# Masked decay products and FFN weight preparation of a Mamba-2 + NVFP4 kernel moved from GpSimd to ScalarE, VectorE and TensorE

## The reference

```
zxbcdt = u @ W_in                      # 256 -> z 512, x 512, B 128, C 128, dt 8
xBC = silu(causal_conv4(xBC))          # 4 taps along the tokens
dt = softplus(dt + dt_bias); A = -exp(A_log); dA = A * dt       # one per token and head
L = exp(segsum(dA))                    # decay between tokens, lower triangle
y = (C B^T * L) @ (x * dt)  + what earlier tokens leave behind  + D * x
y = rmsnorm(y * silu(z)) @ W_out;  h = layernorm(u + y)
W[k] = LUT[4-bit code] * scale[block of 32]                     # gate, up (2048x256), down (256x2048)
out = layernorm(h + (gelu(h @ Wg.T) * (h @ Wu.T)) @ Wd.T)
```

## Time and profile before

| | |
|---|---|
| median of 3 runs | 1005.04 us (1004.16 to 1058.38) |
| the profiled execution | 1005.52 us, its span 1003.8 us |
| TensorE busy | 920.3 us, 92% of the span |
| VectorE busy | 722.4 us, 72% |
| ScalarE busy | 457.8 us, 46% |
| GpSimd busy | 268.1 us, 27% |
| start to 85 us | the first group |
| 85 to 205 us | group 0 with the first group's MLP (front half to 130 us) |
| 205 to 868 us | groups 1 to 6, 110 to 111 us each |
| 868 to 1004 us | the last group, and its MLP |

### The profile page before, as it was taken

The page is one execution under the profiler, slowest core; times in us unless marked ns, Lnnn a source line. Parts: engine busy times, 40 slices in busy tenths (PEclk is TensorE's granted clock), DMA queues, the critical chain, the costliest instruction groups (busy, mean ns, idle before and its releaser), DMA issues.

```text
span 1003.8 us, 15853 instructions
## 1 busy us (share of the span) xinstructions
PE 920.3 (92%) x5416; PEld 803.8 (80%) x5416; DVE 722.4 (72%) x1334; ACT 457.8 (46%) x788; POOL 268.1 (27%) x264
## 2 busy tenths in 40 slices
PE   5558678899999999999999999999999999999997
PEld 4437577888888889888888888888888889978887
DVE  7957867687767876687758786687859766776453
ACT  4534334454544445354545445445445554444332
POOL 4633643203412133203402232203411322111000
PEclk9797778999999999999999999999999999999999
DMA  4011100010001000010001000010001000000000
GB/s 134 26 55 57 36 1 9 15 53 1 1 22 43 21 0 21 0 63 0 0 21 62 1 0 21 0 63 0 21 0 63 1 1 12 25 29 1 1 33 11
DMA packets 18793, 23.11 MB, mean 23 GB/s; under 512 B 1728, under 2 KB 15296, under 8 KB 18752
## 3 DMA queue, kind: packets, MB, share of 16 engines
q1 hardware_dynamic: 18176, 22.56, 7.1%
q10 hardware_dynamic: 576, 0.03, 0.0%
HBM read 14.19 MB, written 4.19 MB: 18 GB/s over the span
## 4 chain that ended last, share of the span: by engine, by line
PE 43%; issue 34%; POOL 13%; DVE 7%; ACT 1%; DMA 1%; POOLq 0%; SPq 0%; DVEq 0%; ACTq 0%
POOL uT_lo L1103 4%; PE mixer L471 4%; PE mixer L472 4%; PE mixer L473 4%; PE up_bank L471 3%; PE gate_bank L471 3%; PE up_bank L472 3%; PE up_bank L473 3%; PE gate_bank L473 3%; PE gate_bank L472 3%; PE mixer L550 3%; PE down L471 2%; PE down L472 2%; PE down L473 2%; POOL uT_hi L1103 2%
## 5 line engine op out<-in xcount | busy, mean ns | idle before, releaser
L471 PE MATMUL down<-wd_hi,in_hi 128*128 128x256 f32 x512 | 145.7, 285 | 0.7 <-DVE in_lo L1000 0.7
L1103 POOL TENSOR_TENSOR uT_hi<-tri,dA_hi 128x1024 fp32r<-128x1024 f32 x30 | 59.2, 1973 | 323.5 <-DVE dA_lo L867 182.1
L472 PE MATMUL down<-wd_lo,in_hi 128*128 128x256 f32 x512 | 145.2, 284 | 0.0
L473 PE MATMUL down<-wd_hi,in_lo 128*128 128x256 f32 x512 | 145.0, 283 | 0.0
L883 DVE SCALAR_TENSOR_TENSOR xbc<-mixer,chan,xbc 128x510 f32<-128x510 f32 (+1 forms) x162 | 110.9, 685 | 27.1 <-ACT xbc L680 24.7
L738 ACT ACTIVATE in_hi<-act_sb 128x512 fp32r<-128x512 f32 (+1 forms) x144 | 83.6, 581 | 94.1 <-PE down L473 55.5
L752 ACT ACTIVATE act_sb<-gate_bank 128x512 f32<-128x512 f32 (+1 forms) x144 | 79.2, 550 | 103.1 <-PE gate_bank L473 101.3
L471 PE MATMUL up_bank<-hT_hi,wu_hi 128*128 128x512 f32 (+1 forms) x288 | 109.2, 379 | 11.2 <-DVE act_sb L1014 11.2
L471 PE MATMUL gate_bank<-hT_hi,wg_hi 128*128 128x512 f32 (+1 forms) x288 | 116.7, 405 | 2.3 <-ACT act_sb L752 2.3
L1000 DVE TENSOR_TENSOR in_lo<-act_sb,in_hi 128x512 fp32r<-128x512 f32 (+1 forms) x144 | 107.0, 743 | 15.7 <-ACT in_hi L738 15.7
L1014 DVE SCALAR_TENSOR_TENSOR act_sb<-up_bank,act_sb 128x512 f32<-128x512 f32 (+1 forms) x144 | 90.1, 625 | 31.6 <-PE up_bank L473 25.7
(11 more groups left out here) (205 smaller groups left out, 2078.2 us busy)
## 6 DMA issues: line engine op xcount, KB each, us to landing
xbc<-in_u_t_dram SPq DMA_DIRECT2D x7, 512.0 KB, 3.6
h_sb<-in_u_dram SPq DMA_DIRECT2D x7, 512.0 KB, 3.9
h_res<-h_sb SPq DMA_DIRECT2D x7, 512.0 KB, 2.9
out_dram<-h_res SPq DMA_DIRECT2D x7, 512.0 KB, 2.9
scales<-in_ffn_s_dram SPq DMA_DIRECT2D x24, 128.0 KB, 2.2
packed<-in_ffn_w_dram SPq DMA_DIRECT2D x8, 96.0 KB, 2.0
xbc<-in_u_t_dram SPq DMA_DIRECT2D x2, 256.0 KB, 2.8
xbc<-in_W_in_dram SPq DMA_DIRECT2D x1, 512.0 KB, 6.2
```

Source lines behind the costliest of these rows:

```text
L471: nc.tensor.matmul(dst, lh, rh, start=first, stop=False, skip_group_check=True)
L472: nc.tensor.matmul(dst, lh, rl, start=False, stop=False, skip_group_check=True)
L473: return nc.tensor.matmul(dst, ll, rh, start=False, stop=last, skip_group_check=True)
L1103: ins = tt(R, mask, f32(step[:, i, :]).unsqueeze(2).to_broadcast([P, H, P]), ALU.mult)
```

## The change

ScalarE forms both parts of the masked dA, each by eight copies of 128x128 with a scale taken from `dA_hi` or `dA_lo` (16 for a tile, 512 in all); GpSimd's two instructions for a tile go. TensorE now waits for two semaphores, `R_h` and `R_l`. VectorE multiplies codes and scales (`value`) for all 24 chunks. The rest of chunks 12 to 23 is formed as that of the first 12 is, by TensorE (in bank `OB[1]`, the second bank of the down products) and ScalarE. The tables of steps are written anew. GpSimd keeps the lower part of uT, the small steps of the norms and the splits of `W_in`'s z part and of `W_out`, the latter two now in four pieces each, the z part only after the first tap of x4.

```diff
-                elif kind == "R":
-
-                    if i:
-                        wait_ready(pool, f"D{i - 1}b", g)
-                    elif kind_of(g) != "first":
-                        wait_ready(pool, "z3" if tiles(g) == 4 else "x3", g)
-                    wait(pool, dA_ok, g, 1)
-                    mask = tri[:, :].unsqueeze(1).to_broadcast([P, H, P])
-                    for R, step in zip(R_of(g), (dA_hi, dA_lo)):
-                        ins = tt(R, mask, f32(step[:, i, :]).unsqueeze(2).to_broadcast([P, H, P]), ALU.mult)
-                    ins.then_inc(R_ok.sem, 1)
...
+                elif kind == "R":
+                    wait_R(act, i, g)
+                    for R, step, done in zip(R_of(g), (dA_hi, dA_lo), (R_h, R_l)):
+                        for h in range(H):
+                            ins = nc.scalar.activation(R[:, h, :], tri[:, :], ACT.Copy, scale=f32(step[:, i, h:h + 1]))
+                        ins.then_inc(done.sem, 1)
...
-                    wait(pe, R_ok, g, i + 1)
+                    wait(pe, R_h, g, i + 1)
+                    wait(pe, R_l, g, i + 1)
...
+            def value(c):
+
+                block, third = c // 3, c % 3
+                code = codes[:, block % 2, :, :].bitcast(FP8)[:, :, third * CW:(third + 1) * CW]
+                dve.wait_ge(decoded.sem, block + 1)
+                dve.wait_ge(scales_in[c % 2].sem, 16 * (c // 2 + 1))
+                if c >= 2:
+
+                    dve.wait_ge(wt_rest.sem, c - 1)
+                if c == BESIDE_FIRST + 1:
+
+                    wait_ready(dve, "Y1", FIRST)
+                tt(chunk_out(c), code, scales[:, c % 2, :].unsqueeze(1).to_broadcast([P, 2, CW]),
+                   ALU.mult).then_inc(valued.sem, 1)
...
-            def rest(c):
-                hi, lo = prep_dst(c)
-                pool.wait_ge(wt_hi.sem, c + 1)
-                tt(lo, chunk_out(c), f32(hi), ALU.subtract).then_inc(wt_lo_pool.sem, 1)
...
-VALUE = {FIRST: {"x5": [2], "R0": [3], "R1": [4, 5, 6, 7, 8, 9, 10, 11]},
...
+VALUE = {FIRST: {"x0": [2], "x1": [3], "x2": [4], "x3": [5], "D0": [6], "XT0": [7], "XT1": [8], "Y1": [9],
+                 "gT0": [10], "op0": [11]},
...
```

More of the change, by code:

```diff
@@ L57 @@
[L57 to L63, removed]
+BESIDE_FIRST = 12
+DECODE = {FIRST: {"x1": [2], "XT0": [3], "gT0": [4]}, 0: {"x5": [5], "x1": [6], "x3": [7]}}
@@ new lines @@
+VALUE = {FIRST: {"x0": [2], "x1": [3], "x2": [4], "x3": [5], "D0": [6], "XT0": [7], "XT1": [8], "Y1": [9],
+                 "gT0": [10], "op0": [11]},
+         0: {0: [12], "x0": [13], 1: [14], "z1": [15], "x2": [16], 3: [17], "z3": [18], "CB0": [19], 5: [20],
+             6: [21], "XT1": [22], "D1": [23]}}
+UPPER = {FIRST: {"x1": [2], "z0": [3], "z1": [4], "CB0": [5], "D1": [6], "Y0": [7], "Y1": [8], "gT0": [9],
+                 "op0": [10], "gT1": [11]},
+         0: {"x5": [12], "z0": [13], "x1": [14], 2: [15], "z2": [16], "x3": [17], 4: [18], "XT0": [19], "D0": [20],
+             "Y0": [21], 7: [22], 8: [23]}}
@@ new lines @@
+TAKE_OFF = {FIRST: {"x5": [0], "x0": [1], "z0": [2], "x2": [3], "x3": [4], "D0": [5], "Y0": [6], "XT1": [7],
+                    "gT0": [8], "op0": [9], "gT1": [10], "op1": [11]},
+            0: {"x0": [12], 1: [13], "z1": [14], "x2": [15], 3: [16], "z3": [17], "CB0": [18], 5: [19], 6: [20],
+                "XT1": [21], "D1": [22], "Y1": [23]}}
+LOWER = {FIRST: {"x1": [0], "z0": [1], "z1": [2], "x3": [3], "CB0": [4], "D1": [5], "XT1": [6], "Y1": [7],
+                 "op0": [8], "gT1": [9], "op1": [10], "ln1": [11]},
+         0: {"z0": [12], "x1": [13], 2: [14], "z2": [15], "x3": [16], 4: [17], "XT0": [18], "D0": [19], "Y0": [20],
+             7: [21], 8: [22], "XT2": [23]}}
@@ L317, in wait_bank, with wait_R @@
                 wait(eng, s, g - 1, k)
+        def wait_R(eng, i, g):
+            if i:
+                wait_ready(eng, f"D{i - 1}b", g)
+            elif kind_of(g) != "first":
+                wait_ready(eng, "z3" if tiles(g) == 4 else "x3", g)
+            wait(eng, dA_ok, g, 1)
         def f32(ap):
@@ L623, in prep @@
             def prep(g, item):
[L624 to L627, removed]
+                for c in TAKE_OFF[g].get(item, ()):
+                    b = chunk_bank(c)
                     pe.wait_ge(valued.sem, c + 1)
                     if c >= 4:
-                        pe.wait_ge(wt_lo_act.sem, c - 3)
+                        pe.wait_ge(wt_lo.sem, c - 3 if c < BESIDE_FIRST else c)
                     nc.tensor.matmul(b[:, :], ident[:, :], chunk_out(c), start=True, stop=False, skip_group_check=True)
@@ L768, in prep @@
                     upper(c)
-                if kind_of(g) == "first":
-                    for c in LOWER.get(item, ()):
-                        lower(c)
+                for c in LOWER[g].get(item, ()):
+                    lower(c)
             def any_mixer(name, g):
@@ L1045, in decode @@
                 tt(lower, word, lower, ALU.bitwise_or).then_inc(decoded.sem, 1)
+            def value(c):
[9 more added lines that the diff above has]
+                   ALU.mult).then_inc(valued.sem, 1)
             def prep(g, item):
+                for c in VALUE[g].get(item, ()):
+                    value(c)
                 for b in DECODE[g].get(item, ()):
@@ L1058, in _ @@
             decode(0)
+            value(0)
+            value(1)
             dve.wait_ge(win_top.sem, 1)
@@ L1153, in any_mixer @@
                     pool.wait_ge(wout_top.sem, 1)
[L1154 removed]
+                    for j in range(JT):
+                        tt(wout_lo[:, j, :], wout_raw[:, j, :], f32(wout_hi[:, j, :]), ALU.subtract)\
+                            .then_inc(wout_ok.sem, 1)
                 mixer(name, g)
```

69 lines of the change are left out of this document (21 added, 48 removed).

## The result

The changed kernel takes **1009.7 us** (median of 6 runs, 1009.1 to 1010.0) against 1006.4 of the kernel before (median of 6, which counts a slow run of 1058.4 us; the five others have a median of 1005.5): the ratio without that run is 1.0035, with a 95% interval from 1.0018 to 1.0052. 984 us were forecast, in a range from 970 to 1009. The profiled execution has a span of 1007.4 us, 3.6 us more than before's 1003.8.

What follows compares the result with a forecast made beforehand. TensorE bounds steady groups, VectorE's queue, held up by GpSimd, group 0's front half. From 1005.5 us: 2 (first 85 us), 10 and 6 (group 0's front half, head part) and 3.5 (steady groups) off, 984 us; range 970 to 1009.

Steps and rivals of the forecast that it cites:

- R's price: ScalarE's scaled 128-column copies for R: 0.30 us apart, 4.8 us a tile, bounds 0.22 and 0.40 us a copy.
- Rivals 1 and 2: ScalarE's R copies: not overlapping, 0.40 us each, 1010 us (chance 0.14); or ScalarE bounding the head part, about 1040 us (0.06).
- So a steady group gets 0.5 us shorter: Steady groups: the wait for W shrinks with R on ScalarE; six groups and the last one gain 3.5 us.
- TensorE still busy over 98% of a steady group: Sign in the new profile's steady groups; below 97% ScalarE's queue, and the prediction with it, would be priced wrong.
- the four rivals: Whole kernel: copies not overlapping (0.14), ScalarE bounding the head part (0.06), group 0 hardly gaining (0.22), everything gaining (0.12).
- The front half of group 0, -10: Group 0 before its head part: VectorE's queue relieved by net 9.5 us, 10 us gained, bounds 3 and 14.
- 14 matmuls of 0.23 us, 3 us, go into its 14 us of waits: Group 0's front half: TensorE's added chunk matmuls, 3 us, would fit inside its existing waits.
- rival 3: Group 0 hardly gains, as chunks go round in-order engines and TensorE stops at each: 3 us and 0 there, 998 us; chance 0.22.
- The head part of group 0, -6: Group 0's later part: earlier W and faster Y, less 4 us for R1 and chunk steps; 6 us gained, bounds 0 and 9.
- The first 85 us, -2: Start of the kernel: VectorE freed of GpSimd, against new products and R on ScalarE; 2 us gained, bounds 6 gained, 3 lost.
- R0 and R1 eat 5 to 7 of it: First 85 us: convolutions end 6 us earlier, and the first group's R copies on ScalarE use up 5 to 7 us.

Runs made afterwards that it cites:

- after_pad64: The changed kernel with 128 long-satisfied waits (64 instructions) ahead of VectorE's first wait for the channels, no loop instruction altered; 1001.9 us.
- best: The changed kernel with the first group's R on GpSimd, rests of chunks 12 to 23 subtracted by VectorE, and spare waits spread over idle places; 981.5 us.
- r_only: The kernel before with R made by ScalarE's 16 copies a tile, the chunks staying with GpSimd; 996.9 us.

## Why the prediction was wrong

All four terms of the sum had the wrong size, two of them the wrong sign. By its own steps:

- **R's price was right.** 0.29 us apart (forecast 0.30), 390 ns long, 4.68 us a tile (4.8); D0 late by 0.56 us (0.5), Y0's wait gone, VectorE's `in_lo`, `tail` and `xtail` at 0.68, 0.17 and 0.69 us. The budget of the Trainium skill's page "ScalarE: Activation LUTs", section "Rules for kernel authors", which comes to an estimated 0.41 us, is near what the row shows as a duration, 0.39 us; as a distance it is 0.12 us too much. Rivals 1 and 2 didn't happen.
- **"So a steady group gets 0.5 us shorter"** was right for every second group and a quarter of the truth for the others. The step failed in counting the wait for W as its 1.42 us alone; the windows of before show 1.7 us of slow clock behind it in every second group. Without the idle stretches (after_pad64) groups 1 to 6 take 659.1 instead of 667.3 us: 8.2 us where I had 3.
- **"TensorE still busy over 98% of a steady group"** (97.6% was measured) failed on something that I had not priced at all. I took the groups that the diff doesn't touch as changed by R only. The chunk products moved VectorE's loop in its program, and it was fetched again at each turn: 4 times some 2.1 us, and 1.7 us more in group 5, where TensorE's granted clock was 0.91 on average for 20 us (667 to 687) around the wait. Together 669.1 - 659.1 = 10.0 us. This is the largest single part of the miss, and it isn't in any of the four rivals.
- **The front half of group 0, -10.** VectorE's relief came as worked out (cut by stage from 42.6 to 32.5 us busy, 10.0 where I had 9.5), and TensorE's two waits for it, 14 us, went to 1. What failed is the sentence that TensorE's "14 matmuls of 0.23 us, 3 us, go into its 14 us of waits". A take-off is 1.1 us at the full clock and 2.27 at the low one, where I had 0.46, so that the six of this half take 8.0 us, and 8.3 us of waits for the lower part stand in place of the old ones. TensorE's idle time fell by 7.0 us and its busy time rose by 3.9. It was rival 3, to which I gave 0.22 with this very mechanism: it had -3 here, and -3.2 was measured.
- **The head part of group 0, -6.** The 8.1 us of waits for W are down to 0.2, as forecast. The chunks took them and 3.5 us more: 6.8 us of waits at three take-offs (4.12 us of them at 147.83, where the lower part stands behind R1's 4.7 us and an upper part), 1.8 us at D2 and 7.9 us of take-offs. TensorE's idle time rose by 1.5 us and its busy time by 2.1. Without take-offs and bank this part takes 66.5 us (best). Rival 3 had 0 here; +3.5 was measured.
- **The first 85 us, -2.** "R0 and R1 eat 5 to 7 of it" was 10.5 us of waits, since R0 can't start before the convolutions and `cb` on ScalarE are through, and GpSimd's copy had long been done. VectorE's last step of the convolutions ended 2.1 us earlier (38.2 instead of 40.3), not 6. With R on GpSimd the stage ends 2.9 us earlier than before, which is the forecast's -2 and its upper half.

Without the placement's effect and the first group's R the changed kernel would be at an estimated 1009.7 - 10.0 - 6.2 = 993.5 us; what is left above best is 12 us, the length that group 0 has too much (122.4 against 109.9 us). So three steps failed: the unpriced fetches of the loop (10.0 us), the take-offs hidden for nothing in group 0, and R's place in the first group's queue (the stage came out 5.3 us over its forecast). Why the fetches come at one position and not at another is only bounded: VectorE's loop is fetched again where it begins at instruction 415 or 427 and not at 367, 463 and 479; ScalarE's with its R in it at 316 and not at 328, 332, 349 and 361. Which size of block lies behind that I have not tested.

## What to carry to other kernels

Cost an edit in the engines' instruction streams, too: instructions added ahead of a loop can make the unchanged loop stand at each turn, seen as idle time without a releaser on one engine and as packets of an instruction queue that come in multiples of the turns. Relief of the engine that sets a stretch is worth little where the new path of the work puts time on the next engine: here 12 small take-offs took back 12 us of TensorE or more, beside the waits of a ring through in-order queues and one buffer. Price each stop of the new path from rows of the same instruction, and compare idle and busy time of the stage apart, since waits that go can come back under another name. And a short wait of TensorE can cost more than its length where the clock falls behind it, so look at the windows behind each wait before it is priced.

## What the runs showed of the hardware

- Instruction fetch in a loop: 39 packets of 8,192 bytes instead of 19, VectorE or ScalarE idle for 1.7 to 2.7 us once a turn, 59 with both; it comes and goes with 12 to 64 instructions ahead of the loop.
- VectorE's product of two SBUF operands (`in_lo`) took 1.65 us beside GpSimd's product and 0.68 without it; its products that read a matmul's result (lines 917 and 919, 348.85 and 349.45 us) took 0.68 us beside it too.
- The take-off of a chunk (two records of 128x512 in f32 and one more product) held TensorE for 1.1 us at full clock and 2.27 at 0.50.
- A gap of 1.42 us of TensorE was followed by 8 us at 0.93 and 0.64 of the clock in every second group of the kernel before; gaps of 0.57 us in r_only were not in any of groups 2 to 6.
- 64 instructions of satisfied waits take 6.3 us on VectorE, 0.1 us each.
- Sixteen scaled copies of 128x128 on ScalarE, scale from SBUF, stand 0.29 us apart, each 0.39 us long.
